# Conv-attention, linear attention and routed experts on one core: row lists pre-filled, table registers read at once, GpSimd left with the power, weights copied by VectorE, a new instruction order

## What is computed

```python
# L0, per image: n = 256 tokens
q, k, v = wq @ xf + bq, wk @ xf + bk, wv @ xf
sim = softmax(q^T k / sqrt(64) + key_mask, axis=2)
x = x + gamma * (v @ sim^T)
# L1 attention: linear, cos/sin weighted, cumulated over the 8 images; 8 heads of 16
t = tokens(x)
q, k, v = relu(ln(t) @ q_w.T + q_b), relu(ln(t) @ k_w.T + k_b), ln(t) @ v_w.T + v_b
t = t + (cumulated q.(k v) / max(q.k, EPS)) @ out_w.T + out_b
# L1 experts: 2 of 8 for each of the 2048 tokens
probs = softmax(ln(t) @ router_w); combine = top-2 weights, normalized
t = t + sum_e combine_e * ((silu(ln(t) @ w1_e) * (ln(t) @ w3_e)) @ w2_e)
```

## Time and profile before

| | us |
|---|---|
| runs of the kernel | 198.16 median (197.84 to 201.89, 3 runs) |
| profiled execution, its own time | 198.26 |
| its span in the trace | 196.5 |
| busy: TensorE | 145.5 (74% of the span) |
| busy: VectorE | 100.9 (51%) |
| busy: ScalarE | 97.4 (50%) |
| busy: GpSimd | 100.4 (51%) |

### The profile page before, as it was taken

The page is one execution under the profiler, slowest core; times in us unless marked ns, Lnnn a source line. Parts: engine busy times, 40 slices in busy tenths (PEclk is TensorE's granted clock), DMA queues, the critical chain, the costliest instruction groups (busy, mean ns, idle before and its releaser), DMA issues.

```text
span 196.5 us, 4178 instructions
## 1 busy us (share of the span) xinstructions
PE 145.5 (74%) x1113; PEld 126.6 (64%) x1113; DVE 100.9 (51%) x400; ACT 97.4 (50%) x294; POOL 100.4 (51%) x142
## 2 busy tenths in 40 slices
PE   1899999999687978763998808866499989892000
PEld 1478886887476756452997808856399979791000
DVE  2177377789329699885156830234045445320163
ACT  3298986878387737131356502433235655552000
POOL 0003340727868688678068777756116746756000
PEclk9999999999969999996699985999889999999555
DMA  6989200000000000139442158661342332110595
GB/s 172 315 251 415 100 2 0 0 3 27 27 29 19 29 27 17 54 96 286 131 126 95 54 142 300 186 203 50 84 95 66 89 77 67 34 42 0 163 273 207
DMA packets 17925, 21.37 MB, mean 109 GB/s; under 512 B 3355, under 2 KB 14304, under 8 KB 17646
## 3 DMA queue, kind: packets, MB, share of 16 engines
q1 hardware_dynamic: 14910, 16.38, 27.8%
q0 software_dynamic: 2272, 4.24, 6.3%
q10 hardware_dynamic: 720, 0.49, 0.9%
HBM read 15.21 MB, written 6.33 MB: 110 GB/s over the span
## 4 chain that ended last, share of the span: by engine, by line
PE 45%; DMA 13%; POOL 12%; issue 11%; SPq 9%; DVE 6%; ACT 2%; POOLq 0%; DVEq 0%; ACTq 0%
PE ps L879 14%; PE ps L894 7%; POOL rows_x L502 6%; DMA xb<-rows_x 4%; PE ps L743 3%; SPq L376 3%; PE ps L723 3%; DMA XT<-rows_y 3%; PE ps L868 2%; DMA rows_x<-pad 2%; PE ps L715 2%; PE ps L708 2%; PE ps L707 2%; PE ps L782 2%; DMA X<-in_x_ch 2%
## 5 line engine op out<-in xcount | busy, mean ns | idle before, releaser
L510 POOL DMA_INDIRECT rows_y<-yb,xb x39 | 38.3, 981 | 27.1 <-ACT yb L661 20.2
L502 POOL DMA_INDIRECT rows_x<-xrow,slot x32 | 36.0, 1125 | 17.8 <-issue 10.8
L879 PE MATMUL ps<-xbT,WB 128*128 128x128 f32 x312 | 42.1, 292 | 0.0
L879 PEld LDWEIGHTS ps<-xbT,WB 128*128 128x128 f32 x312 | 40.6, 210 | 0.0
L894 PE MATMUL ps<-W,hid 128*128 x156 | 25.4, 296 | 5.0 <-DVE hid L1194 3.9
L653 ACT ACTIVATE gate<-ps 128x256 f32<-128x256 f32 x39 | 14.9, 383 | 22.3 <-PE ps L879 19.6
L894 PEld LDWEIGHTS ps<-W,hid 128*128 128x128 f32 x156 | 21.2, 201 | 6.8 <-issue 6.6
L1194 DVE TENSOR_TENSOR hid<-gate,ps 128x256 f32<-128x256 f32 x39 | 16.0, 414 | 18.0 <-ACT gate L653 15.2
L1207 DVE COPY WB<-W 128x512 f32 x22 | 10.2, 462 | 24.5 <-PE ps L879 21.5
L661 ACT ACTIVATE yb<-ps,xb 128x128 f32<-128x128 f32 x39 | 14.4, 368 | 12.6 <-PE ps L894 11.1
L868 PE MATMUL ps<-CF,xb 128*128 128x128 f32 x39 | 9.1, 296 | 11.6 <-DMA xb<-rows_x 10.9
(11 more groups left out here) (141 smaller groups left out, 294.6 us busy)
## 6 DMA issues: line engine op xcount, KB each, us to landing
WB<-in_w SPq DMA_DIRECT2D x17, 256.0 KB, 3.4
xb<-rows_x SPq DMA_DIRECT2D x39, 65.0 KB, 2.0
W<-in_w SPq DMA_DIRECT2D x1, 2048.0 KB, 10.4
X<-in_x_ch SPq DMA_DIRECT2D x8, 128.0 KB, 3.7
XT<-in_x_tok SPq DMA_DIRECT2D x8, 128.0 KB, 3.7
W<-in_w SPq DMA_DIRECT2D x1, 1024.0 KB, 12.5
XT<-rows_y SPq DMA_DIRECT2D x4, 192.0 KB, 4.5
X<-rows_y SPq DMA_DIRECT2D x4, 192.0 KB, 4.6
```

Source lines behind the costliest of these rows:

```text
L502: pool.indirect_dma_start(rows_x, bass.IndirectOffsetOnAxis(ap=slot[:, g:g + 1], axis=0), xrow[:, i * T + t, c, :], None, bounds_check=DUM ...
L510: pool.indirect_dma_start(rows_y, bass.IndirectOffsetOnAxis(ap=xb[:, n, DEST_COL:ROW].bitcast(I32), axis=0), yb[:, n, :], None, bounds_che ...
L879: last = pe.matmul(bank(BANK_GU[s])[:, k * P:(k + 1) * P], WB[:, s % WBS, k * P:(k + 1) * P], xbT[:, s % XBT, :], start=True, stop=True)
```

## The change

1. **Row lists.** `pad_lists`, `pad_row` and the 8 transfers with computed places are gone. Instead SP issues eight fixed transfers behind the input loads; transfer c fills rows 256c to 256c+255 of all 8 lists (1.06 MB each, 8.5 MB in all) out of a padding tile that now holds four rows per partition. A scatter of image i waits for transfer i; the third table's loads wait for all eight. W13 and W2 are loaded behind the first of them.
2. **Registers.** Each table is read with one read per engine (9, 8 and 22 registers), on SP right behind the table and ahead of the waits for the scatters, on TensorE and VectorE at a named place in their order (`read_experts`).
3. **Norms.** GpSimd does the power alone. VectorE adds the epsilon (`lin_spread`, `route_spread`) and makes mean times rstd (`lin_shift`, `route_shift`).
4. **Small products first.** TensorE starts with 24 bf16 products of a tile of ones, 128 x 128, before the first loads have landed. The tile of ones is VectorE's first instruction.
5. **Weights.** All 39 weight blocks are copied by VectorE; SP loads none.
6. **Order.** All five lists and the bank tables are new.

```diff
-READ = 8
+READ = 26
+PACK = 4
+WARM_MATMULS = 24
...
+            def fill_rows(c):
+                here = rows_x[0:E * CAP, :].rearrange("(e r) d -> e (r d)", e=E)[:, c * N * ROW:(c + 1) * N * ROW]
+                sp.dma_start(here.rearrange("e (p k) -> p e k", k=PACK * ROW),
+                             pad[0:N // PACK, :].unsqueeze(1).broadcast_to([N // PACK, E, PACK * ROW])).then_inc(filled[c], 16)
+            fill_rows(0)
             sp.dma_start(W13[:, :], w13).then_inc(ld_w13, 16)
             sp.dma_start(W2[:, :], w2).then_inc(ld_w13, 16)
...
+            for c in range(1, B):
+                fill_rows(c)
...
             for k, (_, blocks, first) in enumerate(TABLES):
-                if k == len(TABLES) - 1:
-                    pad_lists()
                 sp.wait_ge(table_done, k + 1)
+                read_table(sp, first_row, T_ROW, k)
...
                 for s in range(first, first + blocks):
                     load_rows(s)
-                    if k < len(TABLES) - 1:
-                        load_weights(s)
...
-                pool.wait_ge(mv1_done, 2 * (i + 1))
+                pool.wait_ge(ve1_done, i + 1)
...
+                    pool.wait_ge(nb1_done, i - 1)
-                pool.tensor_scalar(nm1[:, b, :], mv1[:, b, :, 0], -1.0, None, ALU.mult)
-                link(pool.tensor_scalar(ve1[:, b, :], mv1[:, b, :, 1], LN_EPS, None, ALU.add))
-                link(pool.tensor_tensor(rs1[:, b, :], ve1[:, b, :], CF[:, C_HALF:C_HALF + T], ALU.pow))
-                pool.tensor_tensor(nb1[:, b, :], nm1[:, b, :], rs1[:, b, :], ALU.mult).then_inc(rs1_done, 1)
+                pool.tensor_tensor(rs1[:, b, :], ve1[:, b, :], CF[:, C_HALF:C_HALF + T], ALU.pow).then_inc(rs1_done, 1)
...
+                    pool.wait_ge(filled[i], 16)
...
+            pe.wait_ge(ones_ready, 1)
+            for _ in range(WARM_MATMULS):
+                pe.matmul(bank(BANK_CV[0])[:, 0:P], ONES[:, :], ONES[:, :], start=True, stop=True)
```

More of the change, by code:

```diff
@@ L279, in hybrid_block @@
         warm_ready = sem("warm_ready")
-        pool_done = sem("pool_done")
+        ones_ready = sem("ones_ready")
+        filled = [sem(f"filled{c}") for c in range(B)]
+        ve1_done = sem("ve1_done")
+        nb1_done = sem("nb1_done")
+        nb2_done = sem("nb2_done")
         rs1_done = sem("rs1_done")
@@ L358, in pieces, with read_table @@
             return sum(len(halves(i)) for i in range(n))
[L360 to L378, removed]
+        def read_table(eng, registers, line, k):
+            _, blocks, first = TABLES[k]
+            for s in range(first, first + blocks, READ):
+                m = min(READ, first + blocks - s)
+                eng.reg_load(registers[s:s + m], table[line:line + 1, s:s + m])
         @block.sync
@@ L432, in _ @@
                 if k == len(TABLES) - 1:
-                    sp.wait_ge(pads_stored, 16 * (E + 1))
+                    sp.wait_ge(pads_stored, 16)
+                    for c in range(B):
+                        sp.wait_ge(filled[c], 16)
                 for s in range(first, first + blocks):
                     load_rows(s)
-                    if k < len(TABLES) - 1:
-                        load_weights(s)
             for n in range(RING):
@@ L692, in _ @@
+            silu(37); weigh(36); silu(38); weigh(37); weigh(38)
         @block.tensor
@@ L881, in gate_up, with read_experts @@
                 last.then_inc(gu_done, 1)
-            expert_of = table_reader(pe, T_EXPERT, E - 1)
+            expert_of = [pe.alloc_register(f"pe_expert{s}") for s in range(BLOCKS)]
+            def read_experts(k):
+                pe.wait_ge(table_done, k + 1)
+                read_table(pe, expert_of, T_EXPERT, k)
             def down(s):
@@ new lines, in _ @@
+            turn_x(0); turn_x(1); lin_proj_v(7); route_rank(4); route_turn(5); lin_out_turn(6); route_logits(5)
+            gate_up(0); lin_scores(7, 0); turn_x(2); lin_out(6); lin_scores(7, 1); route_rank(5); table_count(1)
+            down(0); gate_up(1); lin_scores_turn(7); turn_x(3); gate_up(2); table_turn(1); turn_x(4); gate_up(3)
+            down(1); turn_x(5); turn_x(6); turn_x(7); turn_x(8); read_experts(1); down(2); lin_out_turn(7)
+            down(3); lin_out(7); gate_up(4); gate_up(5); gate_up(6); route_turn(6); down(4); down(5)
@@ new lines, in _ @@
+            route_logits(6); down(6); gate_up(7); turn_x(9); route_rank(6); route_turn(7); gate_up(8)
+            route_logits(7); down(7); turn_x(10); gate_up(9); route_rank(7); table_count(2); down(8); turn_x(11)
+            gate_up(10); turn_x(12); gate_up(11); turn_x(13); gate_up(12); table_turn(2); down(9); down(10)
+            down(11); turn_x(14); down(12); gate_up(13); turn_x(15); gate_up(14); turn_x(16); gate_up(15)
+            down(13); down(14); gate_up(16); down(15); read_experts(2); down(16); turn_x(17); turn_x(18)
@@ new lines, in _ @@
+            gate_up(17); turn_x(19); gate_up(18); turn_x(20); down(17); gate_up(19); down(18); turn_x(21)
+            turn_x(22); gate_up(20); down(19); turn_x(23); gate_up(21); down(20); turn_x(24); gate_up(22)
+            turn_x(25); down(21); gate_up(23); turn_x(26); down(22); gate_up(24); turn_x(27); down(23)
+            gate_up(25); turn_x(28); down(24); turn_x(29); gate_up(26); down(25); turn_x(30); gate_up(27)
+            down(26); turn_x(31); gate_up(28); turn_x(32); down(27); gate_up(29); turn_x(33); down(28)
@@ L935, in _ @@
+            gate_up(30); turn_x(34); down(29); gate_up(31); turn_x(35); down(30); gate_up(32); turn_x(36)
+            down(31); gate_up(33); turn_x(37); down(32); gate_up(34); turn_x(38); down(33); gate_up(35)
+            down(34); gate_up(36); down(35); gate_up(37); down(36); gate_up(38); down(37); down(38)
         @block.vector
@@ new lines, in _ @@
+            weights(7); weights(8); hidden(5); weights(9); hidden(6); weights(10); route_shift(7); weights(11)
+            route_top(6); route_index(6); route_gap(6); route_mask(6); route_seen(6); weights(12)
+            route_where(6); route_weights(6); route_slots(6); hidden(7); weights(13); route_top(7); hidden(8)
+            route_index(7); route_gap(7); route_mask(7); route_seen(7); route_weights(7); weights(14)
+            route_where(7); table_rows(2); route_slots(7); hidden(9); hidden(10); hidden(11); weights(15)
@@ L1249, in _ @@
+            weights(35); hidden(30); weights(36); hidden(31); weights(37); hidden(32); weights(38); hidden(33)
+            hidden(34); hidden(35); hidden(36); hidden(37); hidden(38)
             for q in range(PARTS):
```

348 lines of the change are left out of this document (162 added, 186 removed).

## The result

| | before | changed |
|---|---|---|
| median of 4 runs each, same chip | 198.92 (197.84 to 201.89) | 184.66 (184.52 to 188.02) |
| ratio, 95% interval | 1 | 0.929 (0.922 to 0.935) |

The time lies in the forecast's own range (177 to 188), 2.2 us above the forecast.

The account below looks back on a forecast made before the run. No engine bounds the whole span; TensorE's holes between 50 and 142.7 us can be won. Third table at 110, plus 17.5 to block 17, 34.3 and 19.0, plus 1.8 around the span: 182.6, called 182.5; own range 177 to 188.

Parts of the forecast that it names:

- The bound: No engine bounds the whole span; TensorE's 25.7 us idle between 50 and 142.7 us can be won.
- T2: Moment when the third table is turned, decided by VectorE: forecast 110 us, 114.1 before.
- The chain piece from 128.3 to 135.8 goes: Fillers behind the third table, from issue to last landing, leave the chain because fixed transfers replace them.
- one behind the other on the path: Before block 17, VectorE's then TensorE's read of 22 registers, 5.1 us each, both delay block 17.
- I take most of it as gone, a sixth left: Of VectorE's 21.9 us idle between 50 and 114 us, a sixth remains, giving 110 for the third table.
- The 2 us taken off at the start: Small products raise TensorE's clock before the first real products, saving 2 us (bounds 0 and 2.5).
- The second rival: VectorE becomes the bound, half its idle stays: third table turned at 117.3, time 190; chance 0.18.
- The first gate_up near 80: Sign expected in the new profile: the first blocks' gate_up product starts near 80 us.
- The bound of 0: Lower bound on the small products' gain at the start: the clock rises no earlier, 0 us.
- the 7.9 us that the forecast held possible: Possible GpSimd cost if 17 weight copies on VectorE, 0.46 us each, shut out its descriptor writes; nothing was charged.
- I take the nearest kind, the later reads on the same table: Reading 22 registers at once costs 0.21 us a register on SP, 0.23 on TensorE and VectorE.
- The first rival: Quicker: big register read cheap, VectorE without idle, third table at 106.4, block 17 15 us later; 176.5, chance 0.16.

Follow-up runs that it names:

- experiment 10: Changed kernel with tables at columns 0, 16, 32, reads of whole eights, and two GpSimd norms moved between image 3's scatters: 179.08 us, ratio 0.893.
- 9: Changed kernel with tables starting at columns 0, 16 and 32 and reads lengthened to 16, 8 and 24 registers: 177.90 us, ratio 0.887.
- 1: The changed kernel again, unaltered, for a profile (its profiled execution took 185.71 us): 185.12 us, ratio 0.930 to the kernel before.
- 2: Changed kernel without the 24 small products at the start: 185.75 us, ratio 0.933 to the kernel before.
- experiment 4: Changed kernel with the old computed fillers behind the third count instead of the eight fixed transfers: 186.52 us, ratio 0.935 to the kernel before.
- experiment 3: Changed kernel with the three tables starting at columns 0, 16 and 32 instead of 0, 9 and 17: 177.73 us, ratio 0.893.
- experiment 11: As experiment 10, with VectorE's bias_parts moved behind conv_max(1) at the start: 177.49 us, ratio 0.886 to the kernel before.

## Why the forecast held, and where its steps missed

**The bound, and T2 to block 17: right.** "The chain piece from 128.3 to 135.8 goes" and the big reads on VectorE and TensorE stand "one behind the other on the path": both holes are there. The sizes too: 4.8 on SP, 5.5 and 5.1 on the other two, against 4.6 and 5.1. Block 17 stands 16.8 behind T2, not 17.5.

**T2: the sum's most mis-sized piece, 114.85 for 110.** "I take most of it as gone, a sixth left" was too hopeful. From 50 to 114 us VectorE is now busy 52.0 of 64 us and its two reads take 3.0: 86%, not 90. That leaves 9.0 us idle where a sixth was 3.6: 5.4 us more than the sum has. Two more terms missed. The 2 us taken off at the start did not come. And VectorE's new work was put too high: from 50 us to T2 it is busy 52.8 instead of 42.2 us, and with the reads that is 13.6 more, where the sum has 16.2. 5.4 + 2.0 - 2.6 is T2's delay of 4.8; that it is no larger is partly luck. The second rival ("half its idle stays", T2 = 117.3) was nearly as close. Two timelines of the changed kernel show one place of the idle time. First GpSimd's timeline at image 3's scatters:

```profile
69.77 2.20 POOL L473 DMA_INDIRECT rows_x<-xrow,slot  x1 [1.32 <-DVE slot L1137]
72.28 2.27 POOL L473 DMA_INDIRECT rows_x<-xrow,slot  x1 [0.30 <-issue]
...
76.14 0.97 POOL L473 DMA_INDIRECT rows_x<-xrow,slot  x1 [0.30 <-issue]
77.12 0.74 POOL L460 TENSOR_TENSOR rs<-ve,CF 128x2 f32<-128x2 f32 x1
```

and VectorE's at the same moments:

```profile
69.23 1.20 DVE L1043 TENSOR_TENSOR num<-vt,sco 128x1024 f32<-128x1024 f32 x1
...
71.51 1.20 DVE L1006 TENSOR_TENSOR qk<-kT,qT 128x1024 f32<-128x1024 f32 x1
...
77.90 0.16 DVE L1075 SCALAR_TENSOR_TENSOR nb<-mv,rs 128x2 f32<-128x2 f32 x1 [2.67 <-POOL rs L460]
```

Two scatters beside large products of VectorE took 2.20 and 2.27 instead of 0.97. The norm of another image stands behind all four, VectorE waits 2.67 for its power, and TensorE 3.49 for the row that is made from it, from 75.8 to 79.3. The Trainium skill (GPSIMD Engine Reference, section Key points) names VectorE instructions with two SBUF inputs as such a contention; the trace agrees, with 1.2 to 1.3 us more for each of these two. The forecast knew this hold-up from the earlier trace rows, charged it to the weight copies (rightly at nothing), and didn't ask which scatters would meet the large products in the new order. That this place set T2 is not shown: experiment 10 moved the norm ahead of two of the scatters, and T2 came 1.9 us later than in 9.

**"The first gate_up near 80": it was 87.0.** The scatters of images 0 to 3 were done at 77.1, forecast 75. Their landing, the first row load and the steps that stand before `gate_up(0)` on TensorE took 10 us, where 5 had been allowed.

**Small products: 2 taken, 0.4 found** by the timelines of 1 and 2, nothing in the medians that can be told. The rate did not come up by the time the first real products ran. The bound of 0 was the nearer end.

**Norms: right in size.** The power alone is 0.69 to 0.74 us by its medians where four operations took 1.69; VectorE's new ones are 0.15 to 0.17 each. Putting them back costs 5.5 to 5.7 us; in the profiles T2 comes 4.9 later by it and block 17 5.2.

**Weights: copying was a gain of 3.4 to 4.1**, not only work for VectorE. The forecast counted 6.9 us on VectorE and named SP's issues between the row loads without giving them a price. These issues, together with SP's two added reads, cost more than the copies do. GpSimd's result scatters have a mean of 1.0 us beside the 39 copies. A copy that ran wholly within one (at 140.30 for 0.43 us, the scatter at 139.83) left it at 1.02, so the 7.9 us that the forecast held possible did not show and nothing was the right charge.

**Row lists: right, hidden.** No scatter waits for a fill, which ends at 60, not 67, at 200 to 206 GB/s between 32 and 55 us. In the sum, however, the fillers' 7.5 us and the reads' 10 us are parallel branches: with the reads in place, taking the fillers out was worth 1.4, not to be told from nothing (experiment 4).

**Registers: the price was right, the reason wrong.** "I take the nearest kind, the later reads on the same table" gave 0.21 to 0.23 a register and 0.22 to 0.25 came out for the 22. The first two reads of the earlier trace rows were cheap not as first ones but since the eight registers began at column 0. The Trainium skill (Runtime: NRT & Kernel Launch, section Instruction fetch mechanics) has some 200 ns a register even in bulk, for loads from HBM. The table here lies in SBUF: reads from columns 9 and 17 come near that figure, with 0.22 to 0.26, while from 16 and 32 it is 0.065 to 0.09 (experiments 3 and 9). The first rival, a cheap big read, is thus a second version of this kernel: 177.7 where it said 176.5, but with T2 at 113.3, not 106.4, and block 17 at T2 + 10.3, not 15.

**What fills the gap.** The misses were +4.85 at T2, -0.7 to block 17, -0.5 and -0.5 behind it: together +3.1, the 185.7 of the profiled run against 182.6.

The fastest versions are 3, 9 and 11, 177.5 to 177.9 us, 11% under the kernel before and 4% under the changed one. What was left open: whether the fillers would cost more with the cheap reads, experiment 11 without 10's move, and why the clock falls by as much as it does around 80 us.

## What to carry to other kernels

When a row of a profile shows two prices for one operation, find what differs between the two before you take the nearer one: here it was a start column, and it was worth as much as half the whole change. Add up parallel branches as a maximum, not a sum: the fill was worth 6.5 us alone and at most a little beside the reads. And when work moves between engines, look not only at how much each has, but at which queued instruction meets which: behind one short power that stood after four scatters, VectorE waited 2.67 us and TensorE 3.49. Then try the move before you believe in its worth: the one of experiment 10 won nothing.

## What was not expected of the hardware

- A register read from SBUF: 22 registers from column 17 took 4.8 to 5.5 us in the changed kernel and 4.6 to 6.5 over all runs, from column 32 1.9 to 2.0, and 24 from column 32 1.6 to 1.8. Eight from column 9: 1.9 to 2.1; from 16: 0.61 to 0.67.
- 24 small bf16 products right before the first real ones left these at the lower rate: two took 1.12 us at 4.2 us and four 0.61 only from 9.8. In the profile's page the clock of these slices reads 9, as for full speed, so for the start the lengths of the products are what tells the rate.
- A hole of 2 to 4 us in TensorE cost more than itself: the eight products of block 17 behind it took 2.05 where they take 1.13 behind the shorter hole of experiment 3.
